# Shared expert: the last 64 gate rows and 64 up rows in one stationary operand, and TensorE's loop over tiles written out

## The chip, the core and the metric

The kernel runs on one core of one Trainium2 chip. The time is the device time of one execution in microseconds (us). Three runs of the kernel before took 1300.08, 1300.76 and 1302.69 us, median 1300.76 us. All other times below come from one profiled execution of it.

## The reference

The layer has four stages, each with a layer norm ahead of it and a residual sum behind it: a state-space mixer, a feed-forward block (FFN), a gated linear attention, and the same FFN a second time with the same weights. The FFN is where the change is:

```python
x = hidden_states.reshape(-1, H)                                        # 1024 tokens x 256
shared = _silu_and_mul(x @ shared_gate_up_w.T) @ shared_down_w.T        # 704 gate rows, 704 up rows; 704 hidden
shared = shared * jax.nn.sigmoid(x @ sgate_w.T)
routing_weights = jax.nn.softmax(x @ gate_w.T, axis=-1)                 # 16 experts
topk_w, topk_ids = jax.lax.top_k(routing_weights, TOP_K)                # 4 per token
# for each expert e: acc += silu_and_mul(x @ w13_e.T) @ w2_e.T * coef_e
out = shared + sparse_out
```

`_silu_and_mul` takes the first half of the rows as gate g, the second half as up u, and gives silu(g) * u. All of it is float32.

## The kernel before

The five instruction streams (SP for DMA issue, POOL = GpSimd, ACT = ScalarE, DVE = VectorE, PE = TensorE) are written by hand, one function for each stage and engine, and keep order among each other by counting semaphores. Float32 products with full accuracy are made of three matmuls: each operand is split into a rounded high part and a low rest, and `mm3` adds hi*hi, hi*lo and lo*hi into one PSUM bank.

**The shared expert.** The 704 hidden rows are cut into tiles of 128 (`S_TILES` = 6); 704 = 5.5 x 128, so the sixth tile (number 5) is half empty and is filled up with zero rows. The tokens are cut into two chunks of 512. For each tile and chunk PE computes the gate product into PSUM bank c and the up product into bank 2 + c, each by 2 (halves of the 256 features) x 3 matmuls of 128x512 (`f_up_pe`, L1084; `f_up_part_pe`, L1078). ACT takes silu of the gate bank into `f_s` (L1288), DVE multiplies by the up bank into `f_h` (L1545), ACT rounds it to `fh_hi`, DVE makes the rest `fh_lo` (L1549), and PE multiplies with the down weights: 4 blocks of 128 tokens x 3 matmuls of 128x256 for each tile and chunk, summed over the six tiles in banks 4 to 7 (`f_down_pe`, L1095). Up of tile i + 1 runs on PE before down of tile i. Tiles 0 and 1 are written out among the routing's matmuls; tiles 2 to 5 are two rounds of a hardware loop (`pe.Fori`, L1071).

**Routing and experts.** Beside it DVE computes which tokens go to which expert. With that POOL scatters the token rows into slots in DRAM by 32 indirect DMAs (L1335, destination `slots_d`), SP waits for their landing and loads the slots back tile by tile (`xg`, L1579), and PE works through 47 tiles of tokens (`f_experts_pe`, L1106): transpose (L1147), up (L1170), transpose of the hidden (L1183), down (L1195). SP waits for 8 scatters more ahead of each of tiles 0 to 3, so tile 3 is loaded only when all 32 have landed. PE's order puts the transpose of tile t + 1 ahead of up of tile t, so tile 3's transpose (row L1147) stands ahead of everything else of tiles 2 and later. Behind the experts come the residual sum and the next stage, or the end.

Of the kernel before, what the change touches and what calls it, by code (L numbers as in the profile page):

```python
# [23 lines left out]
ALU = mybir.AluOpType  # L24
ACT = mybir.ActivationFunctionType
AX_X = mybir.AxisListType.X

P = 128
BATCH, SEQ, DM = 4, 256, 256
# [3 lines left out]
CHUNKS = TOKENS // CHUNK  # L33
# [61 lines left out]
def build_layer(nc, xT, consts, a_vg, a_dt, a_heads, a_wo, a_par, ffn_w, router_w, route_c, moe_up, moe_down, b_qk, b_vo, b_conv,  # L95
                b_bg, b_par, out):
    ctx = ExitStack()
    with ctx:
        sems = {}

        def sem(name):
            if name not in sems:
                sems[name] = ctx.enter_context(nc.semaphore(name))
            return sems[name]
# [166 lines left out]
        def f32(ap):  # L271
            return ap.bitcast(F32)
# [14 lines left out]
        def at(t, *idx):  # L287

            return tuple(v[idx] for v in t[:2])
# [11 lines left out]
        def cols(c):  # L301
            return slice(c * CHUNK, (c + 1) * CHUNK)
# [119 lines left out]
        def split_hi(dst, src, hi_sem):  # L422
            return nc.scalar.copy(dst[0], src).then_inc(sem(hi_sem), 1)  # L423
# [632 lines left out]
        def f_pe(pe, n, f):  # L1056

            f_up_part_pe(pe, 0, 1, 1).then_inc(sem("f_up_done"), 1)
            f_up_pe(pe, f, 1, [0])

            routed(pe, "dve", f, "sofar")
            nc.tensor.matmul(ps[:, COUNT_BANK, COUNTS], ones, sofar[:, :, BLOCKS - 1], start=True, stop=True,
                             skip_group_check=True).then_inc(sem("f_route_pe"), 1)
            nc.tensor.matmul(ps[:, ROUTE_BANK, RANKS], after, mask, start=True, stop=False, skip_group_check=True)
            nc.tensor.matmul(ps[:, ROUTE_BANK, RANKS], ones, sofar[:].rearrange("p e b -> p b e"), start=False, stop=True,
                             skip_group_check=True).then_inc(sem("f_route_pe"), 1)
            f_down_pe(pe, f, 0, [0])
            f_up_pe(pe, f, 1, [1])
            routed(pe, "dve", f, "ranks_read")
            f_down_pe(pe, f, 0, [1])  # L1070
            with pe.Fori(0, S_TILES // 2 - 1) as pair:  # L1071
                for j in range(2):
                    f_up_pe(pe, f, 2 * pair + 2 + j, p=j)
                    f_down_pe(pe, f, 2 * pair + 1 + j, p=1 - j)
            f_down_pe(pe, f, S_TILES - 1)
            f_experts_pe(pe, f)

        def f_up_part_pe(pe, p, c, s):  # L1078

            for k in range(KT):  # L1080
                ins = mm3(ps[:, 2 * s + c, :], at(fgu, slice(None), p, k, s), at(xn, slice(None), k, cols(c)), k == 0, k == KT - 1)
            return ins

        def f_up_pe(pe, f, i, chunks=range(CHUNKS), p=None):  # L1084

            first = isinstance(i, int) and i == 0
            gu_split(pe, f, i)
            for c in chunks:
                if not first:
                    pe.wait_ge(sem("f_h"), HIDDENS * f + 2 * i + c - 1)  # L1090
                for s in range(2):
                    ins = f_up_part_pe(pe, i % 2 if p is None else p, c, s)
                ins.then_inc(sem("f_up_done"), 1)

        def f_down_pe(pe, f, i, chunks=range(CHUNKS), p=None):  # L1095

            p, only = (i % 2, i) if p is None else (p, None)
            d_split(pe, f, i)
            for c in chunks:
                pe.wait_ge(sem("f_h_split"), HIDDENS * f + 2 * i + c + 1)  # L1100
                for t in range(CHUNK_BLOCKS):
                    ins = mm3(ps[:, 4 + 2 * c + t // 2, t % 2 * DM:(t % 2 + 1) * DM], at(fh, slice(None), p, block_of(c, t)),
                              at(fd, slice(None), p), only == 0 and t % 2 == 0, only == S_TILES - 1)
                ins.then_inc(sem("f_down_done"), 1)

        def f_experts_pe(pe, f):  # L1106
# [178 lines left out]

        def f_silu_act(act, f, i, c):
            act.wait_ge(sem("f_up_done"), HIDDENS * f + 2 * i + c + 1)
            nc.scalar.activation(f_s[:, c], ps[:, c, :], ACT.Silu).then_inc(sem("f_silu"), 1)  # L1288

        def f_hi_act(act, f, i, c):  # L1290
            act.wait_ge(sem("f_h"), HIDDENS * f + 2 * i + c + 1)
            split_hi(at(fh, slice(None), i % 2, cols(c)), f_h[:, c], "f_h_hi")

        def f_prepare_act(act, f):
            act.wait_ge(sem("f_rw_loaded"), 16 * f + 16)
# [246 lines left out]

        def f_h_dve(dve, f, i, c):
            dve.wait_ge(sem("f_silu"), HIDDENS * f + 2 * i + c + 1)
            nc.vector.tensor_tensor(f_h[:, c], f_s[:, c], ps[:, 2 + c, :], ALU.mult).then_inc(sem("f_h"), 1)  # L1545

        def f_lo_dve(dve, f, i, c):
            dve.wait_ge(sem("f_h_hi"), HIDDENS * f + 2 * i + c + 1)
            nc.vector.tensor_tensor(fh[1][:, i % 2, cols(c)], f_h[:, c], f32(fh[0][:, i % 2, cols(c)]),  # L1549
                                    ALU.subtract).then_inc(sem("f_h_split"), 1)  # L1550

        def f_tile_sp(sp, i):
# [773 lines left out]
def _layout(i):  # L2326
    c = np.ascontiguousarray
    i = {k: np.asarray(v) for k, v in i.items()}
    w = i["L0_attn_a_W_in"]
    hn = A_HEADS * A_STATE  # L2330
    bc = w[2 * A_INNER:2 * A_INNER + 2 * hn].reshape(2, A_HEADS, A_STATE, KT, P)
    vg = w[:2 * A_INNER].reshape(2, A_TILES, P, KT, P)
    par = [i["L0_attn_a_conv_w"].reshape(A_TILES, P, A_TAPS).transpose(1, 0, 2).reshape(P, -1),
           i["L0_attn_a_conv_b"].reshape(A_TILES, P).T, i["L0_attn_a_D_param"].reshape(A_TILES, P).T,
           np.tile(i["L0_attn_a_A_log"], 4)[:, None], np.tile(i["L0_attn_a_dt_bias"], 4)[:, None]]


    gu = np.zeros((S_TILES, 2, P, DM), np.float32)
    dn = np.zeros((S_TILES, P, DM), np.float32)
    sg = i["L0_ffn_shared_gate_up_w"].reshape(2, S_HIDDEN, DM)  # L2340
    sd = i["L0_ffn_shared_down_w"].T
    for t in range(S_TILES):
        n = min(P, S_HIDDEN - t * P)
        gu[t, :, :n] = sg[:, t * P:t * P + n]
        dn[t, :n] = sd[t * P:t * P + n]
    gu = gu.reshape(S_TILES, 2, P, KT, P).transpose(0, 4, 3, 1, 2).reshape(S_TILES, P, KT * 2 * P)
    rw = np.zeros((P, DM), np.float32)
    rw[:EXPERTS] = i["L0_ffn_gate_w"]
    rw[GATE_ROW] = i["L0_ffn_sgate_w"][0]
    up = i["L0_ffn_w13"].reshape(EXPERTS, 2 * E_HIDDEN, KT, P).transpose(3, 0, 2, 1)  # L2350
    down = np.zeros((HALF_E, EXPERTS, E_STRIDE), np.float32)
    down[:, :, :2 * DM] = i["L0_ffn_w2"].reshape(EXPERTS, DM, 2, HALF_E).transpose(3, 0, 2, 1).reshape(HALF_E, EXPERTS, 2 * DM)

    qk = np.stack([i["L0_attn_b_Wq"], i["L0_attn_b_Wk"]]).reshape(2, B_HEADS, B_KD, KT, P)
    v = i["L0_attn_b_Wv"].reshape(B_HEADS, B_VT, P, DM).transpose(0, 2, 1, 3)
    cv = np.stack([i["L0_attn_b_Wq_conv"], i["L0_attn_b_Wk_conv"]]).reshape(2, B_HEADS, B_KD, P, B_TAPS)
    cb = np.stack([i["L0_attn_b_bq_conv"], i["L0_attn_b_bk_conv"]], axis=1)
    wo = i["L0_attn_b_Wo"].reshape(DM, B_HEADS, B_VT, P).transpose(1, 3, 2, 0)
    reps = P // B_HEADS
    bg = np.stack([np.tile(i["L0_attn_b_Wb"], (reps, 1)), np.tile(i["L0_attn_b_Wg"], (reps, 1))])  # L2360
    bpar = [np.tile(i["L0_attn_b_bb"], reps)[:, None], np.tile(i["L0_attn_b_bg"], reps)[:, None]]
    return dict(
        xT=c(i["L0_attn_a_x"].reshape(BLOCKS, P, DM).transpose(1, 0, 2)),
        consts=_constants(),
        a_vg=c(vg.transpose(4, 1, 3, 0, 2)),
        a_dt=c(_feature_major(np.tile(w[2 * A_INNER + 2 * hn:], (4, 1)))),
        a_heads=c(bc.transpose(1, 4, 3, 0, 2)).reshape(A_HEADS * P, KT * 2 * P),
        a_wo=c(i["L0_attn_a_W_out"].T),
        a_par=c(np.concatenate(par, axis=1)),
        ffn_w=c(np.concatenate([gu, dn], axis=2)).reshape(S_TILES * P, KT * 2 * P + DM),  # L2370
        router_w=c(rw.reshape(P, KT, P).transpose(2, 1, 0)),
        route_c=_route_constants(),
        moe_up=c(up).reshape(P, EXPERTS * E_STRIDE),
        moe_down=c(down).reshape(HALF_E, EXPERTS * E_STRIDE),
        b_qk=c(qk.transpose(1, 4, 3, 0, 2)).reshape(B_HEADS * P, QKW),
        b_vo=c(np.stack([v, wo], axis=2)).reshape(B_HEADS * P, VOW),
        b_conv=c(np.concatenate([cv.transpose(1, 3, 0, 4, 2).reshape(B_HEADS * P, CONVW), cb], axis=1)),
        b_bg=c(bg.reshape(2, P, KT, P).transpose(3, 2, 0, 1)),
        b_par=c(np.concatenate(bpar, axis=1)),
    )  # L2380
# [13 lines left out]
```

## Time and profile before

| | |
|---|---|
| device time, three runs | 1300.08, 1300.76, 1302.69 us |
| span of the profiled execution, first to last instruction | 1256.4 us |
| what lies around the span (median of the runs less that span) | 44.4 us |
| PE busy | 1205.8 us, 96% of the span |
| DVE, ACT, POOL busy | 847.7, 814.3, 773.7 us |
| first FFN: shared expert and routing, experts | 380 to 437.7 us, 437.7 to 568 us |
| second FFN: shared expert and routing, experts | 1064 to 1119.7 us, 1119.7 to 1241 us |

The profile gives the span of its execution, not that execution's device time; the rest is the difference to the median. "PEclk" in a row is the granted clock of TensorE as a share of its full 2.4 GHz, so 0.50 is 1.2 GHz. A number in square brackets behind a row is how long the engine was idle ahead of it, and on whom it waited.

### The profile page before, as it was taken

Reading aid. Unit: us, or ns where it says so; the run is one execution under the profiler, and the core shown is the slowest. Engines: PE = TensorE matmul, PEld = TensorE weight load, DVE = VectorE, ACT = ScalarE, POOL = GpSimd, SP = SyncE. Lnnn points to the kernel's source line nnn. Section 1 sums busy time; section 2 is a strip of 40 time slices with the busy share of each in tenths; the row PEclk is TensorE's granted clock in tenths of the full one; section 3 lists DMA queues with packets and bytes.
Section 4 is the critical chain, followed back from the end, with each engine's and each line's share of the span. In section 5 each row is a group of like instructions: output and inputs, shape, how many; then the busy total and the mean of one; then the engine's idle time right before and its main releaser. Section 6 shows DMA issues by size and latency. Waiting matters only on the chain. (4 is left out here: it accounts for less than half of the span.)

```text
span 1256.4 us, 23651 instructions
## 1 busy us (share of the span) xinstructions
PE 1205.8 (96%) x7571; PEld 1057.3 (84%) x7572; DVE 847.7 (67%) x2088; ACT 814.3 (65%) x1782; POOL 773.7 (62%) x648
## 2 busy tenths in 40 slices
PE   6999999999989999997999999999999998999997
PEld 5888888888877867775899999999999997877775
DVE  7777777777788533358777777777777777743335
ACT  5887777787765333343887887888888775433332
POOL 3456665667543746552677777777777764465663
PEclk9999999999999999998999999999999998999999
DMA  3355745754215957761222232222122211776666
GB/s 114 86 145 152 206 108 164 185 144 124 54 49 162 328 123 128 138 131 61 64 66 62 61 72 75 58 71 63 58 58 62 63 20 43 254 264 115 112 116 145
DMA packets 94279, 141.60 MB, mean 113 GB/s; under 512 B 8184, under 2 KB 73976, under 8 KB 93048
## 3 DMA queue, kind: packets, MB, share of 16 engines
q1 hardware_dynamic: 74400, 102.32, 29.6%
q0 software_dynamic: 15744, 20.98, 9.8%
q10 hardware_dynamic: 4056, 17.30, 4.1%
q8 instruction: 42, 0.69, 0.2%
q14 instruction: 37, 0.30, 0.1%
HBM read 99.71 MB, written 40.86 MB: 112 GB/s over the span
## 5 line engine op out<-in xcount | busy, mean ns | idle before, releaser
L1341 POOL DMA_INDIRECT sums_d<-e_y,xg x88 | 137.2, 1560 | 98.3 <-DMA sums_d<-e_y,xg 45.0
L427 POOL TENSOR_TENSOR ms_a<-m_a,ms_a 128x384 fp32r<-128x384 f32 x128 | 130.2, 1017 | 97.5 <-ACT ms_a L423 97.3
L1462 DVE COPY e_hT<-ps 88x256 f32<-88x256 f32 x94 | 39.5, 420 | 136.3 <-PE ps L1183 134.8
L1170 PE MATMUL ps<-w,e_xT 128*128 (+1 forms) x376 | 127.6, 462 | 1.5 <-ACT e_xT L1255 1.0
L894 DVE TENSOR_TENSOR m_a<-ps,e_a 128x384 f32<-128x384 f32 x128 | 71.2, 557 | 67.2 <-PE ps L278 66.2
L276 PE MATMUL ps<-xn_hi,aw_hi 128*128 128x512 f32 x256 | 107.0, 418 | 1.0 <-DVE bmat_lo L817 1.0
L278 PE MATMUL ps<-xn_hi,aw_lo 128*128 128x512 f32 x256 | 101.0, 395 | 0.0
L277 PE MATMUL ps<-xn_lo,aw_hi 128*128 128x512 f32 x256 | 100.8, 394 | 0.0
L427 POOL TENSOR_TENSOR qk_lo<-qf,qk_hi 128x512 fp32r<-128x512 f32 x64 | 84.4, 1340 | 25.2 <-ACT qk_hi L423 23.6
L427 POOL TENSOR_TENSOR ms_b_lo<-m_b,ms_b_hi 128x384 fp32r<-128x384 f32 x64 | 65.2, 1019 | 52.4 <-ACT ms_b_hi L423 52.4
L1195 PE MATMUL ps<-w,e_hT 88*128 (+1 forms) x376 | 96.7, 379 | 0.0
L1335 POOL DMA_INDIRECT slots_d<-rows,slot_i x64 | 66.0, 1031 | 42.8 <-DVE slot_i L1527 23.9
L427 POOL TENSOR_TENSOR planes_lo<-qsum,planes_hi 128x256 fp32r<-128x256 f32 x64 | 57.8, 904 | 47.6 <-ACT planes_hi L1829 47.0
L1170 PEld LDWEIGHTS ps<-w,e_xT 128*128 128x128 f32 x376 | 64.0, 190 | 23.2 <-issue 2.0
L423 ACT CAST ms_a<-m_a 128x384 fp32r<-128x384 f32 x128 | 64.9, 507 | 23.7 <-DVE m_a L894 22.6
L1262 ACT ACTIVATE e_s<-ps 128x176 f32<-128x176 f32 x94 | 29.8, 318 | 74.2 <-PE ps L1170 74.2
L827 DVE SCALAR_TENSOR_TENSOR e_a<-rows_a,ncum_a,ps 128x128 f32<-128x128 f32 x256 | 76.6, 341 | 1.9 <-DMA rows_a<-a_rows_d 1.0
L1272 ACT COPY e_y<-ps 128x256 f32<-128x256 f32 x88 | 32.8, 372 | 67.5 <-PE ps L1195 55.2
L276 PE MATMUL ps<-fold_hi,xn_hi 128*128 128x256 f32 x256 | 73.3, 286 | 1.1 <-ACT q L1820 1.1
L276 PE MATMUL ps<-planes_hi,wconv_hi 128*128 128x260 f32 (+1 forms) x256 | 73.3, 286 | 0.2 <-DVE conv_y L1988 0.2
L278 PE MATMUL ps<-planes_hi,wconv_lo 128*128 128x260 f32 (+1 forms) x256 | 73.0, 285 | 0.0
L277 PE MATMUL ps<-planes_lo,wconv_hi 128*128 128x260 f32 (+1 forms) x256 | 72.9, 285 | 0.0
(311 smaller groups left out, 4524.2 us busy)
## 6 DMA issues: line engine op xcount, KB each, us to landing
rows_a<-a_rows_d SPq DMA_DIRECT2D x64, 256.0 KB, 4.8
xg<-slots_d SPq DMA_DIRECT2D x94, 144.0 KB, 2.4
slots_d<-slot_init SPq DMA_DIRECT2D x10, 1152.0 KB, 6.6
w<-moe_up ACTq DMA_DIRECT2D x8, 1408.0 KB
wconv_raw<-b_conv SPq DMA_DIRECT2D x16, 513.0 KB, 3.6
aw_raw<-a_heads SPq DMA_DIRECT2D x32, 256.0 KB, 2.8
wvo_raw<-b_vo SPq DMA_DIRECT2D x16, 512.0 KB, 3.3
rows_b<-b_rows_d SPq DMA_DIRECT2D x32, 256.0 KB, 4.8
```

Of the source, the lines that this page charges most:

```text
L276: nc.tensor.matmul(o, w[0], v[0], start=first, stop=False, skip_group_check=True)
L277: nc.tensor.matmul(o, w[0], v[1], start=False, stop=False, skip_group_check=True)
L278: return nc.tensor.matmul(o, w[1], v[0], start=False, stop=last, skip_group_check=True)
L423: return nc.scalar.copy(dst[0], src).then_inc(sem(hi_sem), 1)
L427: return nc.gpsimd.tensor_tensor(dst[1], src, f32(dst[0]), ALU.subtract).then_inc(sem(done_sem), 1)
L827: ins = nc.vector.scalar_tensor_tensor(e[:, d * P:(d + 1) * P], row[:, d * P:(d + 1) * P], ncum[:, 2 * b + d, bass.ds(h, 1)], causal_ps, A ...
L894: nc.vector.tensor_tensor(m_a[:, b, :], ps[:, 4 + b, 0:TRI], e_a[:, b, :], ALU.mult).then_inc(sem("a_m_done"), 1)
L1170: ins = nc.tensor.matmul(ps[:, 2 + t % 2, 0:2 * E_HIDDEN], e_xT[:, t % 2, k], weights_of(w13, t, at_w, k * 2 * E_HIDDEN, 2 * E_HIDDEN), st ...
L1195: ins = nc.tensor.matmul(ps[:, 6 + t % 2, 0:DM], e_hT[0:HALF_E, t % 2, j], weights_of(w2[0:HALF_E], t, at_w, j * DM, DM), start=j == 0, st ...
L1335: nc.gpsimd.indirect_dma_start(slots_d[f], bass.IndirectOffsetOnAxis(ap=slot4_i[:, b, k:k + 1], axis=0), rows[:, b, :], None).then_inc(sem ...
L1341: nc.gpsimd.indirect_dma_start(sums_d[f][t % CHAINS], bass.IndirectOffsetOnAxis(ap=xg[:, t % XG, ROW_ID:ROW_ID + 1].bitcast(U32), axis=0), ...
L1462: nc.vector.tensor_copy(e_hT[0:HALF_E, t % 2], ps[0:HALF_E, 4 + t % 2, 0:2 * P].rearrange("p (j m) -> p j m", j=2)).then_inc(sem("e_hT"), 1)
```

## The change

Tile 5 now has no zero rows in its up weights. Its 64 gate rows and 64 up rows are put side by side in the first of the two stationary operands of that tile, so that one product gives gate in partitions 0 to 63 of bank c and up in partitions 64 to 127 of the same bank. PE issues 6 matmuls for each chunk of that tile instead of 12. ACT's silu reads partitions 0 to 63 and writes `f_s` at 64 to 127; DVE multiplies partitions 64 to 127 of `f_s` and of the bank, and the two splits work on partitions 64 to 127 too. The 64 down rows move to partitions 64 to 127, with zeros ahead; the down matmuls stay 128x256 and as many as before. Since the last tile is not like the others any more, PE's loop over tiles 2 to 5 is replaced by the same steps written out.

```diff
-            with pe.Fori(0, S_TILES // 2 - 1) as pair:
-                for j in range(2):
-                    f_up_pe(pe, f, 2 * pair + 2 + j, p=j)
-                    f_down_pe(pe, f, 2 * pair + 1 + j, p=1 - j)
+            for i in range(2, S_TILES):
+                f_up_pe(pe, f, i)
+                f_down_pe(pe, f, i - 1)
             f_down_pe(pe, f, S_TILES - 1)
...
-                for s in range(2):
-                    ins = f_up_part_pe(pe, i % 2 if p is None else p, c, s)
+                for s in range(1 if i == S_TILES - 1 else 2):
+                    ins = f_up_part_pe(pe, i % 2, c, s)
...
-            nc.scalar.activation(f_s[:, c], ps[:, c, :], ACT.Silu).then_inc(sem("f_silu"), 1)
+            nc.scalar.activation(f_s[f_rows(i), c], ps[0:HP if i == S_TILES - 1 else P, c, :], ACT.Silu).then_inc(sem("f_silu"), 1)
+
+        def f_rows(i):
+
+            return slice(HP, P) if i == S_TILES - 1 else slice(0, P)
...
-            split_hi(at(fh, slice(None), i % 2, cols(c)), f_h[:, c], "f_h_hi")
+            split_hi(at(fh, f_rows(i), i % 2, cols(c)), f_h[f_rows(i), c], "f_h_hi")
...
-            nc.vector.tensor_tensor(f_h[:, c], f_s[:, c], ps[:, 2 + c, :], ALU.mult).then_inc(sem("f_h"), 1)
+            r = f_rows(i)
+            nc.vector.tensor_tensor(f_h[r, c], f_s[r, c], ps[r, c if i == S_TILES - 1 else 2 + c, :], ALU.mult).then_inc(sem("f_h"), 1)
...
+    gu[S_TILES - 1, 0] = sg[:, S_HIDDEN - HP:].reshape(P, DM)
+    dn[S_TILES - 1, HP:] = sd[S_HIDDEN - HP:]
```

On PE, in the first FFN, the loop was entered behind the last down matmul of tile 0 like this (`fgu` are the up weights, `xn` the normed tokens; what a row waits for stands behind it):

```order
L278 MATMUL ps<-fd_hi,fh_lo 128x256
L1071 UNCONDITIONAL_BRANCH
L1071 ISA
L1090 ISA [waits f_gu_split_dve]
L276 MATMUL ps<-xn_hi,fgu_hi 128x512 [waits f_h]
L277 MATMUL ps<-xn_lo,fgu_hi 128x512
```

The branch, the loop's register and the separate waiting instruction are gone; the first up matmul now waits for both semaphores itself. Inside the loop the second chunk of an odd tile (3, then 5) had 12 matmuls:

```order
L276 MATMUL ps<-xn_hi,fgu_hi 128x512 [waits f_h]
L277 MATMUL ps<-xn_lo,fgu_hi 128x512
L278 MATMUL ps<-xn_hi,fgu_lo 128x512
L276 MATMUL ps<-xn_hi,fgu_hi 128x512
L277 MATMUL ps<-xn_lo,fgu_hi 128x512
L278 MATMUL ps<-xn_hi,fgu_lo 128x512
L276 MATMUL ps<-xn_hi,fgu_hi 128x512
L277 MATMUL ps<-xn_lo,fgu_hi 128x512
L278 MATMUL ps<-xn_hi,fgu_lo 128x512
L276 MATMUL ps<-xn_hi,fgu_hi 128x512
L277 MATMUL ps<-xn_lo,fgu_hi 128x512
L278 MATMUL ps<-xn_hi,fgu_lo 128x512
```

In the changed kernel the second chunk of tile 5 stands on PE with 6 matmuls, and down of tile 4 follows:

```order
L276 MATMUL ps<-xn_hi,fgu_hi 128x512 [waits f_h]
L277 MATMUL ps<-xn_lo,fgu_hi 128x512
L278 MATMUL ps<-xn_hi,fgu_lo 128x512
L276 MATMUL ps<-xn_hi,fgu_hi 128x512
L277 MATMUL ps<-xn_lo,fgu_hi 128x512
L278 MATMUL ps<-xn_hi,fgu_lo 128x512
L276 MATMUL ps<-fd_hi,fh_hi 128x256 [waits f_h_split,f_d_split_dve]
```

Down of tile 4, down of tile 5 and the experts' first transposes stand 12 matmuls nearer in each FFN. On ACT the order is unchanged; the last tile's rows read, in the changed kernel:

```order
L1213 DMA w_208<-moe_down 88x4x512
L1287 ACTIVATE f_s<-ps 64x512 [waits f_up_done] x2
L423 CAST fh_hi<-f_h 64x512 [waits f_h] x2
L1254 COPY e_xT<-ps 128x256 [waits e_turned,f_route_dve]
L1254 COPY e_xT<-ps 128x256 [waits e_turned]
```

Only the height of the two middle rows has changed from 128 to 64 partitions.

## Rows read from the trace of the kernel before

**Rows 1.** The page: busy time, share of the span and instructions of each engine.
```profile
PE 1205.8 (96%) x7571; PEld 1057.3 (84%) x7572; DVE 847.7 (67%) x2088; ACT 814.3 (65%) x1782; POOL 773.7 (62%) x648
```

**Rows 2.** Chain that ended last, second FFN: start, us, what.
```profile
1121.67 2.66 DMA slots_d<-rows,slot_i
...
1126.49 0.44 PE ps L1147 x2
```

**Rows 3.** Timeline of PE, first FFN: start, us, instruction, [idle before <-releaser].
```profile
426.39 0.39 PE L276 MATMUL ps<-xn_hi,fgu_hi 128*128 128x512 f32 x1
...
431.98 0.28 PE L276 MATMUL ps<-fd_hi,fh_hi 128*128 128x256 f32 x1
...
437.73 0.60 PE L1147 MATMUL ps<-const,xg 128*128 128x128 f32 x4
...
439.91 0.43 PE L1147 MATMUL ps<-const,xg 128*128 128x128 f32 x2
...
441.37 0.38 PE L1183 MATMUL ps<-const,e_h 128*88 128x128 f32 x2
444.43 0.44 PE L1147 MATMUL ps<-const,xg 128*128 128x128 f32 x2 [2.68 <-DMA xg<-slots_d]
```

**Rows 4.** Timeline of POOL and of SP's queue, first FFN.
```profile
439.66 0.96 POOL L1335 DMA_INDIRECT slots_d<-rows,slot_i  x1 [0.30 <-issue]
...
435.06 0.32 SPq L1579 DMA_DIRECT2D xg<-slots_d  x1
...
442.48 1.75 SPq L1579 DMA_DIRECT2D xg<-slots_d  x4
```

**Rows 5.** Timeline of PE, second FFN.
```profile
1122.58 0.44 PE L1147 MATMUL ps<-const,xg 128*128 128x128 f32 x2 [0.49 <-DMA xg<-slots_d]
...
1126.49 0.44 PE L1147 MATMUL ps<-const,xg 128*128 128x128 f32 x2 [2.06 <-DMA xg<-slots_d]
```

**Rows 6.** Who PE waited for, 444 to 570, then 1126 to 1252: us, times, longest.
```profile
PE ps L1147 <- DMA xg<-slots_d: 3.3, 2, 2.7
...
PE ps L1147 <- DMA xg<-slots_d: 2.1, 1, 2.1
```

**Rows 7.** Timeline of PE around the loop's way back, first FFN.
```profile
417.82 0.28 PE L278 MATMUL ps<-fd_hi,fh_lo 128*128 128x256 f32 x1
417.94 0.39 PE L276 MATMUL ps<-xn_hi,fgu_hi 128*128 128x512 f32 x1
```

**Rows 8.** Two copies at 32 partitions, two shared-expert steps at 128: ns min/median/max.
```profile
L1284 ACT COPY lgT<-ps x2: 558/566/575, 381.3 to 1063.8; 32x512 f32<-32x512 f32 x2
L1288 ACT ACTIVATE f_s<-ps x24: 589/598/601, 385.9 to 1114.2; 128x512 f32<-128x512 f32 x24
L1366 DVE COPY lgT<-ps x2: 678/678/679, 387.3 to 1069.5; 32x512 f32<-32x512 f32 x2
L1545 DVE TENSOR_TENSOR f_h<-f_s,ps x24: 679/681/690, 386.5 to 1115.9; 128x512 f32<-128x512 f32 x24
```

**Rows 9.** Timeline of PE: three waits in other stages.
```profile
573.80 1.94 PE L342 MATMUL ps<-const,rows 128*128 128x128 f32 x8 [5.47 <-DVE rows L409]
616.71 0.72 PE L276 MATMUL ps<-xn_hi,wqk_hi 128*128 128x512 f32 x1 [1.87 <-ACT q L1820]
1060.83 0.76 PE L281 MATMUL ps<-xn_hi,rw_hi 128*128 128x512 f32 x1 [0.77 <-ACT xn_hi L374]
```

**Rows 10.** Windows: length, PE busy (instructions), PEclk, DMA share, GB/s.
```profile
446.00:448.00 2.00, 2.00 (x12) 1.00 0.13 46
1126.00:1128.00 2.00, 1.51 (x7) 1.00 0.90 258
579.00:579.50 0.50, 0.50 (x3) 0.73 0.00 0
617.00:617.50 0.50, 0.50 (x2) 0.50 0.39 156
1063.50:1064.00 0.50, 0.50 (x3) 0.54 0.00 0
```

More of the change, by code:

```diff
@@ L1082, in f_up_part_pe, with f_up_pe @@
             return ins
-        def f_up_pe(pe, f, i, chunks=range(CHUNKS), p=None):
+        def f_up_pe(pe, f, i, chunks=range(CHUNKS)):
             first = isinstance(i, int) and i == 0
@@ L1090, in f_up_pe, with f_down_pe @@
                     pe.wait_ge(sem("f_h"), HIDDENS * f + 2 * i + c - 1)
-                for s in range(2):
-                    ins = f_up_part_pe(pe, i % 2 if p is None else p, c, s)
+                for s in range(1 if i == S_TILES - 1 else 2):
+                    ins = f_up_part_pe(pe, i % 2, c, s)
                 ins.then_inc(sem("f_up_done"), 1)
-        def f_down_pe(pe, f, i, chunks=range(CHUNKS), p=None):
-            p, only = (i % 2, i) if p is None else (p, None)
+        def f_down_pe(pe, f, i, chunks=range(CHUNKS)):
+            p = i % 2
             d_split(pe, f, i)
@@ L1102, in f_down_pe @@
                     ins = mm3(ps[:, 4 + 2 * c + t // 2, t % 2 * DM:(t % 2 + 1) * DM], at(fh, slice(None), p, block_of(c, t)),
-                              at(fd, slice(None), p), only == 0 and t % 2 == 0, only == S_TILES - 1)
+                              at(fd, slice(None), p), i == 0 and t % 2 == 0, i == S_TILES - 1)
                 ins.then_inc(sem("f_down_done"), 1)
@@ L1544, in f_h_dve @@
             dve.wait_ge(sem("f_silu"), HIDDENS * f + 2 * i + c + 1)
-            nc.vector.tensor_tensor(f_h[:, c], f_s[:, c], ps[:, 2 + c, :], ALU.mult).then_inc(sem("f_h"), 1)
+            r = f_rows(i)
+            nc.vector.tensor_tensor(f_h[r, c], f_s[r, c], ps[r, c if i == S_TILES - 1 else 2 + c, :], ALU.mult).then_inc(sem("f_h"), 1)
         def f_lo_dve(dve, f, i, c):
             dve.wait_ge(sem("f_h_hi"), HIDDENS * f + 2 * i + c + 1)
-            nc.vector.tensor_tensor(fh[1][:, i % 2, cols(c)], f_h[:, c], f32(fh[0][:, i % 2, cols(c)]),
+            r = f_rows(i)
+            nc.vector.tensor_tensor(fh[1][r, i % 2, cols(c)], f_h[r, c], f32(fh[0][r, i % 2, cols(c)]),
                                     ALU.subtract).then_inc(sem("f_h_split"), 1)
@@ L2341, in _layout @@
     sd = i["L0_ffn_shared_down_w"].T
[L2342 to L2345, printed above, removed]
+    for t in range(S_TILES - 1):
+        gu[t] = sg[:, t * P:(t + 1) * P]
+        dn[t] = sd[t * P:(t + 1) * P]
+    gu[S_TILES - 1, 0] = sg[:, S_HIDDEN - HP:].reshape(P, DM)
+    dn[S_TILES - 1, HP:] = sd[S_HIDDEN - HP:]
     gu = gu.reshape(S_TILES, 2, P, KT, P).transpose(0, 4, 3, 1, 2).reshape(S_TILES, P, KT * 2 * P)
```

## The prediction

> **What bounds the kernel now.** I read the busy shares first. PE is busy 96% of the span [rows 1], so 24 matmuls less look like time saved. The share is a mean over stages, though, and the question is which wait ends last behind the shared expert. So next came the chain that ended last, around the second FFN: 32 scatters of POOL, the landing of the last one, the load of a token tile, and only then PE [rows 2]. PE's shared-expert matmuls are not in it. For the first FFN the chain has no pieces, so there I read the timelines. PE ends the shared expert at 437.73, runs the first two expert tiles as far as it may, and then stands 2.68 us, until 444.43, for tile 3 [rows 3]. That tile's load is the first of the four that SP issues from 442.48, behind the last scatter (POOL 439.66 + 0.96 = 440.62) and its landing [rows 4]. In the second FFN PE waits 0.49 us for tile 2 and 2.06 us for tile 3 [rows 5]. Both FFNs are thus held by routing, POOL and DMA, and PE is early by 2.68 us in the one and 2.06 us (2.55 with both waits) in the other.
>
> Behind these waits PE does set the end: over the rest of the experts it waits for a token tile only once more, 3.3 - 2.7 = 0.6 us in the first FFN, and in the second not at all [rows 6]. So what is saved ahead of tile 3's wait is lost in it, and what is lost behind it counts in full.
>
> **Part 1: 12 matmuls less in each FFN.** Up of tile 5 runs from 426.39 to 431.98, where down of tile 4 follows without a gap [rows 3]: 5.59 us for 24 matmuls, 0.233 us each. Half of them go: 12 x 0.233 = 2.80 us for one FFN, 5.59 us for both. PE then reaches the experts at 437.73 - 2.80 = 434.93. Tile 2's transpose can move from 439.91 at most to 437.11; its load is issued at 435.06 [rows 4], so it may become a short wait of its own, which changes nothing behind it. Tile 3 is where it was, at 444.43. PE stands idle from 441.37 + 0.38 - 2.80 = 438.95 on, so 2.68 us become 5.48 us. In the second FFN 0.49 becomes 3.29 us and 2.06 stays. Nothing that the scatters wait for has moved: they depend on logits, counts and ranks, all ahead of the changed code. Gain on the path: 0 of 5.59 us.
>
> **Part 2: the loop written out.** At the loop's way back the next up matmul begins at 417.94, 0.12 us behind the last down matmul at 417.82, with no idle time beside it [rows 7]. Taking the branch away gives 0. The Trainium skill (Runtime: NRT & Kernel Launch, "Instruction fetch mechanics") says that a taken branch whose target lies outside the engine's small instruction window stalls the engine for a fetch. By that rule PE would gain a fetch in each FFN; this case's row shows no such stall here, and the measurement decides. The other way round, written-out code has more instructions to fetch while the weights of the experts load. No row prices that. It is at least nothing, and it would have to exceed 5.48 us in the first FFN or 2.06 + 3.29 = 5.35 us in the second before the end sees it. I take 0.
>
> **Part 3: half-height steps.** Silu, product and the two splits of tile 5 run on 64 partitions instead of 128. Rows of another height bound them: at 32 partitions and the same 512 columns ACT's copy takes 566 ns against 598 for its silu, and DVE's copy 678 against 681 for its product [rows 8]. So height hardly sets the time: between 0 and 0.03 us less each, and I take 0. They all start 2.80 us earlier with the matmul that releases them and stay as far ahead of down of tile 5 as now. Reading gate and up from one bank adds no wait, since silu and product of a chunk already follow each other. If a step took even 1 us longer, the wait at tile 3 would cover it.
>
> **Part 4: the longer idle time and TensorE's clock.** This is the one term that can reach the end. In this execution 2.68 us of idle time left the clock at 1.00 (446 to 448), and the pair of waits in the second FFN did too [rows 10]. Elsewhere 1.87 us of idle time ahead of 616.71 was followed by 0.50 [rows 9, 10]. A wait of 5.47 us, the twin of the new 5.48 us, ends at 573.80 with the clock at 0.50, and the row at 579.0 to 579.5, mean 0.73, puts its return at 579.27: 5.47 us of work at 1.2 GHz instead of 2.4. If PE sets the pace, half of that is lost, 2.7 us. The row of 0.54 at 1063.5 to 1064.0 puts another return at 1063.96, 3.13 us behind 1060.83: 1.6 us lost. A fall of the clock behind tile 3's wait thus costs 1.6 to 2.7 us, 2.1 in the middle.
>
> The Trainium skill (TensorE: Matmul & The Clock Gate, Part 1, "What's actually happening") adds that the monitor's clock runs freely and does not restart with a kernel, so where it switches differs from run to run. No single trace can show that; it agrees with a wait of 1.87 us that lost the clock beside one of 2.68 us that kept it, and by that rule the kernel before pays in some of its runs as well.
>
> What counts is the difference. In the first FFN the changed kernel should pay nearly always; of the kernel before I say half of the executions, since its wait is longer than one that lost the clock but kept it here. That is 2.1 x 1/2 = 1.05 us. In the second FFN both kernels have the 2.06 us wait last, and I take 0, with up to 2.7 us as its other end. As bounds: 0 if both pay alike, 2.7 + 2.7 = 5.4 us if the changed kernel pays twice and the one before never.
>
> **Sum.** Span 1256.4 + 44.4 around it = 1300.8; 0 for matmuls, loop and half-height steps; + 1.05 for the clock: 1301.8 us. The span's rest is taken from the median of the runs, so the sum stands on that median.
>
> **The rivals.**
>
> *The matmuls show at the end (faster).* If something that I take for fixed follows PE (the landing of the scatters, or SP's loads through less pressure on the DMA queues), one stage's or both stages' 2.80 us come back: 1298.0 or 1295.2 us. For it speaks that PE is the busiest engine; against it that no DMA is removed and that both tiles 3 were loaded late while PE stood. Chance 0.12.
>
> *The clock falls behind both waits, and seldom did before (slower).* The place is tile 3's transpose in each FFN, the price 1.6 to 2.7 us each, so 3.1 to 5.4 us together: 1303.9 to 1306.2 us. It decides from the point where PE's idle time in the stage is long enough to lose the clock each time; the twin of 5.47 us speaks for the first FFN, and the profiled execution kept its clock in both. Against it: the kernel before probably pays in part of its runs, and its three times differ by 2.6 us, as much as one such price. Chance 0.26.
>
> *The change does not shorten PE's work (fetch of the longer code, or half-height steps that run late).* Down of tile 5 would then end where it did and the time is 1300.8; were the stall longer than the cover of about 5.4 us, it would be slower by the rest, 1302 or more. Nothing in the profile speaks for it. Chance 0.04, counted as slower.
>
> *My forecast*, no change but for a share of the clock: 0.58.
>
> **How the numbers follow.** A difference under 0.2%, 2.6 us, is about what a measurement of this kernel cannot tell from no change. My forecast's own range is 1299.5 to 1303.5 us, all within it. Faster is the first rival, 0.12. Slower is the second, 0.26, less a little for its lower end within reach of the bound, and the third, so 0.28. Same is the rest, 0.60. For 8 times in 10 I go from 1299.0, which leaves most of the first rival out, to 1305.6, which takes in the second up to near its upper end.
>
> **What would show it.** In the changed kernel's trace: tile 5's up takes 2.80 us, the experts' first transposes begin 2.8 us earlier against the scatters, the wait ahead of tile 3 grows to 5.5 us in the first FFN, and a wait of about 3.3 us stands ahead of tile 2 in the second; the last scatter and the load of tile 3 stand where they stood. The clock is 0.50 behind tile 3's wait in the first FFN, for 3 to 6 us. I am wrong if tile 3's load comes earlier by microseconds, if PE shows gaps in tiles 2 to 5 of the shared expert, or if the clock falls twice and the runs of the kernel before never pay.

## The result and the profile after

The changed kernel is faster. Nineteen runs of it took 1286.83 to 1303.22 us, median 1294.34 us; nineteen of the kernel before took 1298.65 to 1307.22 us, median 1302.69 us. The ratio is 0.9935 (95% interval 0.9918 to 0.9953), the difference of the means 8.2 +- 2.2 us. The forecast of 1301.8 us and its range from 1299.0 us missed it, and faster had been given 0.12.

The page of the changed kernel's profile, its span and the row that answers to [rows 1]:

```profile
span 1295.7 us, 23573 instructions
PE 1207.9 (93%) x7547; PEld 1056.0 (81%) x7548; DVE 847.6 (65%) x2088; ACT 814.0 (63%) x1782; POOL 770.2 (59%) x648
```

This execution's own device time is known: 1297.55 us. So only 1.85 us lie around its span, not 44.4, and its span is 39.3 us longer than that of the kernel before although the kernel is faster. PE's busy time is the same within 0.2%. A second profile of the kernel before (experiment 1) has a span of 1295.0 us in 1296.92 us. The execution that the prediction was read from was an unusual one: with 1.85 us around it, it would have taken 1258 us, and the fastest timed run of the kernel before in this whole study took 1288.97 us.

What the ordinary executions have and the unusual one lacks is seen in PE's waits of the changed kernel from 376 to 470 us (columns: who waited, for what, us in total, times, longest):

```profile
PE ps L278 <- issue: 8.9, 7, 2.4
PE ps L276 <- issue: 6.2, 4, 1.7
PE ps L277 <- issue: 6.2, 4, 2.4
```

"issue" means that no release stands in the profile just ahead of the instruction. No wait for a token tile is in the full list: the 2.68 us of [rows 3] are gone, where the prediction had 5.48 us. The timeline of PE, which answers to [rows 3], shows where these 21.3 us lie:

```profile
415.25 0.49 PE L278 MATMUL ps<-xn_hi,fgu_lo 128*128 128x512 f32 x1
...
417.36 0.28 PE L278 MATMUL ps<-fd_hi,fh_lo 128*128 128x256 f32 x1 [1.12 <-issue]
...
437.80 0.37 PE L278 MATMUL ps<-fd_hi,fh_lo 128*128 128x256 f32 x1 [2.43 <-issue]
439.90 0.37 PE L276 MATMUL ps<-fd_hi,fh_hi 128*128 128x256 f32 x1 [1.73 <-issue]
442.70 0.37 PE L277 MATMUL ps<-fd_lo,fh_hi 128*128 128x256 f32 x1 [2.43 <-issue]
443.42 0.58 PE L278 MATMUL ps<-fd_hi,fh_lo 128*128 128x256 f32 x1 [0.34 <-issue]
...
453.66 0.39 PE L276 MATMUL ps<-xn_hi,fgu_hi 128*128 128x512 f32 x1
...
456.45 0.28 PE L276 MATMUL ps<-fd_hi,fh_hi 128*128 128x256 f32 x1
...
462.20 0.60 PE L1146 MATMUL ps<-const,xg 128*128 128x128 f32 x4
```

From about 416 to 443.4 PE executes a down matmul every 0.7 to 2.8 us, with a few closer together, instead of every 0.12 us. I call this **the stall**. Behind it PE runs the rest of the shared expert without a gap: tile 5's up now takes 456.45 - 453.66 = 2.79 us, as worked out, and the experts begin at 462.20, when the load of tile 3 has long been issued (POOL's last scatter, ACT's silus and SP's queue, which answer to [rows 4] and [rows 8]):

```profile
398.06 1.24 POOL L1338 DMA_INDIRECT slots_d<-rows,slot_i  x1 [11.99 <-DVE slot_i L1530]
...
437.97 0.96 POOL L1338 DMA_INDIRECT slots_d<-rows,slot_i  x1 [0.30 <-issue]
```
```profile
419.83 0.61 ACT L423 CAST fgu_hi<-fw_raw 128x512 fp32r<-128x512 f32 x1
441.31 0.60 ACT L1287 ACTIVATE f_s<-ps 128x512 f32<-128x512 f32 x1 [20.86 <-remote]
...
455.25 0.59 ACT L1287 ACTIVATE f_s<-ps 64x512 f32<-64x512 f32 x1 [0.88 <-PE ps L278]
```
```profile
440.42 2.49 SPq L1584 DMA_DIRECT2D xg<-slots_d  x5
```

POOL's scatters go on at their usual pace through the stall, ACT stands for 20.86 us. The stall begins some 17 us behind the first scatter's begin and ends 443.4 - (437.97 + 0.96) = 4.5 us behind the last one's issue, or 443.4 - 440.4 = 3.0 us behind the landing that lets SP load tile 3.

What ACT waits for can be read. Its silu of a chunk waits for nothing but a semaphore that PE raises with the last up matmul of that chunk. For the second chunk of tile 3 that matmul is the one at 415.25 above; here are the silu in the changed kernel, then matmul and silu of the same chunk in the first profile of the kernel before:

```profile
443.53 0.60 ACT L1287 ACTIVATE f_s<-ps 128x512 f32<-128x512 f32 x1 [1.62 <-remote]
```
```profile
414.85 0.39 PE L278 MATMUL ps<-xn_hi,fgu_lo 128*128 128x512 f32 x1
415.28 0.60 ACT L1288 ACTIVATE f_s<-ps 128x512 f32<-128x512 f32 x1 [1.99 <-PE ps L278]
```

Without the stall the silu begins 0.04 us behind the matmul's end (414.85 + 0.39). With it, 443.53 - 415.74 = 27.8 us pass, and for the first chunk 28.7 us. The trace has an update of this semaphore 0.02 us ahead of each of the two silus, and the profile calls its raiser "remote" because it finds no instruction that raises it then. So PE's signals reach ACT up to 29 us late, and DVE waits for ACT in turn (20.8 us at the longest). Why PE itself issues slowly, this does not show. The window (length, PE, PEld, DVE, ACT, POOL busy with counts, clock, DMA share, GB/s) of the changed kernel, and the same window of the first profile of the kernel before:

```profile
415.00:443.00 28.00, 6.72 (x22) 5.11 (x21) 1.80 (x3) 1.52 (x3) 18.29 (x19) 0.57 0.45 159
1115.00:1143.00 28.00, 8.07 (x20) 5.14 (x20) 0.69 (x1) 0.97 (x2) 17.69 (x19) 0.56 0.45 154
```
```profile
415.00:443.00 28.00, 26.45 (x162) 22.70 (x160) 13.24 (x27) 9.12 (x19) 19.83 (x20) 1.00 0.86 301
```

22 matmuls stand against 162, POOL's scatters are 19 against 20, and the DMA engines move half as much. The granted clock is 0.57 on the mean in place of 1.00. In the chain that ended last, from 1112 to 1165 us in the changed kernel, the shares are these; the landing of scatters and the token tile of [rows 2] have left it, and PE's matmuls behind the stall have come in:

```profile
by line: issue 37.8%; PE ps L276 18.7%; PE ps L277 18.2%; PE ps L278 17.3%; PE ps L1169 5.5%; PE ps L1146 1.3%; ACT e_xT L1254 0.7%; PE ps L1182 0.5%; ACTq L1251 0.0%
```

### The profile page after: what moved, and what is told of

Same layout as the page of the kernel before. It is cut to its first block and busy times, and to the rows that moved or that the text cites. A ratio compares the mean times of both kernels' runs of the same rounds, so it can differ in the third digit from the quotient of the medians.

```text
span 1295.7 us, 23573 instructions
## 1 busy us (share of the span) xinstructions
PE 1207.9 (93%) x7547; PEld 1056.0 (81%) x7548; DVE 847.6 (65%) x2088; ACT 814.0 (63%) x1782; POOL 770.2 (59%) x648
## 5 line engine op out<-in xcount | busy, mean ns | idle before, releaser
L1338 POOL DMA_INDIRECT slots_d<-rows,slot_i x64 | 63.2, 987 | 42.8 <-DVE slot_i L1530 23.9
L427 POOL TENSOR_TENSOR planes_lo<-qsum,planes_hi 128x256 fp32r<-128x256 f32 x64 | 57.7, 901 | 47.0 <-ACT planes_hi L1834 46.3
```

Of the source, the lines that this page charges most:

```text
L427: return nc.gpsimd.tensor_tensor(dst[1], src, f32(dst[0]), ALU.subtract).then_inc(sem(done_sem), 1)
L1338: nc.gpsimd.indirect_dma_start(slots_d[f], bass.IndirectOffsetOnAxis(ap=slot4_i[:, b, k:k + 1], axis=0), rows[:, b, :], None).then_inc(sem ...
```

## The experiments

Twelve experiments ran, in three groups (1 to 4, 5 to 8, 9 to 12), each group on one chip beside its own runs of the kernel before (medians 1296.63, 1298.93 and 1301.93 us). Differences of means are given with a 95% interval.

**1. The kernel before, profiled again** (no edit).

> The kernel before, unchanged, one more profile. The changed kernel's trace shows TensorE issuing one matmul in 1 to 3 us for some 28 us of each shared expert (415 to 443 and 1116 to 1143 us), the profile of before that the prediction was read from does not, and its span was 44 us under the times of its runs. Theory A (an ordinary execution of the kernel before has that stall too, and the profile I read was an execution without it): span 1297 to 1305 us, about 20 us longer in each FFN than in the profile I read, and a clock of 0.50 in each stall. Theory B (the stall belongs to the changed kernel alone, and the 44 us lie outside the span): span about 1256 us again, no stall.

Measured: 1296.92 us, span 1295.0 us. Its window and PE's timeline:

```profile
418.00:444.00 26.00, 12.22 (x29) 5.78 (x27) 1.98 (x3) 1.72 (x3) 17.00 (x18) 0.62 0.38 137
1118.00:1144.00 26.00, 8.80 (x22) 4.53 (x20) 2.67 (x4) 2.09 (x4) 17.03 (x18) 0.61 0.39 139
```
```profile
379.11 0.77 PE L281 MATMUL ps<-xn_hi,rw_hi 128*128 128x512 f32 x1 [0.77 <-ACT xn_hi L374]
...
443.99 0.79 PE L278 MATMUL ps<-xn_hi,fgu_lo 128*128 128x512 f32 x1 [0.81 <-issue]
...
460.33 0.60 PE L1147 MATMUL ps<-const,xg 128*128 128x128 f32 x4
...
1079.72 0.77 PE L281 MATMUL ps<-xn_hi,rw_hi 128*128 128x512 f32 x1 [0.77 <-ACT xn_hi L374]
...
1162.82 0.60 PE L1147 MATMUL ps<-const,xg 128*128 128x128 f32 x4
```

The stall belongs to the kernel before as well. From the router's first matmul (operand `rw_hi`) to the experts 81.2 and 83.1 us pass in the two FFNs; in the first profile it was 59.1 and 58.9. I call this time **the shared expert's time**. So in an ordinary run PE comes late, some 16 us behind tile 3's data, and the 12 matmuls lie behind the stall.

**2 and 7. The loop alone.** The loop is written out, tile 5 stays as before with 24 matmuls.

```diff
-            with pe.Fori(0, S_TILES // 2 - 1) as pair:
-                ...
+            for i in range(2, S_TILES):
+                f_up_pe(pe, f, i)
+                f_down_pe(pe, f, i - 1)
```

> The kernel before with TensorE's loop over tiles 2 to 5 written out, and nothing else; tile 5 keeps its 24 matmuls. Theory A1 (TensorE's work behind the stall sets the end, so the 12 matmuls less in each FFN are the whole gain, and the loop is free): 1302.7, no difference to the kernel before, ratio 0.998 to 1.002. Theory A2 (the loop's own instructions, its branch, register arithmetic and separate waits, are dear while TensorE's instructions come slowly): 2 to 4 us faster, ratio 0.997 or less. Theory C (the longer code costs fetches): slower.

> The kernel before with the loop written out, again, on the chip of this call, to set apart what the loop and what the 12 matmuls are worth. Theory A1: no difference to the kernel before, and 5.6 us slower than the changed kernel. Theory A2 (the loop's own instructions cost in the stall): 2 to 4 us faster than the kernel before.

Measured: ratio 0.9989 (0.9968 to 1.0011) on one chip, 0.9981 (0.9953 to 1.0009) on the other; differences -1.2 +- 2.4 and -3.5 +- 2.5 us (the second without one run of 3051.6 us, which the median of 1297.3 us hardly feels). Neither ratio is told from 1. Weighted together the differences make -2.3 +- 1.7 us, so a small gain is likelier than none. The expectation of no difference (A1) and that of 2 to 4 us (A2) are both still possible.

**3 and 8. The changed kernel, on the same two chips** (no edit).

> The changed kernel again, on the same chip as the others of this call. Expected from its 19 runs: ratio 0.992 to 0.995, 6 to 11 us faster than the kernel before. Theory A1: 5.6 us below loop written out alone (two times 12 matmuls of 0.233 us), more where the clock is 0.50. Theory A2: about 5.6 us below it too, but 8 us below the kernel before.

> The changed kernel on the chip of this call. Theory A1 and A2: 5 to 9 us faster than the kernel before, ratio 0.993 to 0.996.

Measured: medians 1291.79 and 1294.71 us, ratios 0.9975 (0.9950 to 0.9999) and 0.9957 (0.9929 to 0.9985), differences -4.0 +- 2.5 and -5.4 +- 2.9 us. With the first comparison's -8.2 +- 2.2 the weighted mean is -6.1 +- 1.4 us. The 24 matmuls that went make 5.59 us by the prediction's own working. Against the loop alone, though, the changed kernel is ahead by only 2.8 +- 2.8 and 1.9 +- 3.2 us, weighted 2.4 +- 2.1 us, which leaves the expected 5.6 us out. The profiles agree: the shared expert's time is 79.9 to 81.3 us with the loop alone (four FFNs) and 77.1 to 83.6 us in the changed kernel (six). So the sum fits, but that the 24 matmuls count in full is not shown, and the split between tile 5 and the loop stays open.

**4. Scatters behind the shared expert.** POOL waits for the last down product before its first scatter.

```diff
+            pool.wait_ge(sem("f_down_done"), HIDDENS * (f + 1))
             for i, k in enumerate(reversed(range(TOP_K))):
```

> The changed kernel with GpSimd's 32 scatters of an FFN held until TensorE has ended the shared expert. Theory D (the stall is tied to the scatters: it comes while they and their landings run): no stall in the shared expert, which ends some 50 us behind its start as in the profile I read (about 437 us in the first FFN), and TensorE then waits some 40 us for the scatters; span 1300 to 1345 us. Theory E (the stall comes from something else in that stretch, the weights' loads or the code): the stall stays in the shared expert, and the span grows by 35 us or more over the changed kernel's.

Measured: 1328.55 us. No stall is left in the shared expert, whose time in the first FFN is about 56.3 us, the first profile's 59.1 less the 2.8 of tile 5. What takes its place is seen in PE's waits of the first FFN:

```profile
PE ps L1146 <- DMA xg<-slots_d: 38.2, 4, 14.7
```

The stall is tied to the scatters: with none in flight, the same instructions of PE and ACT run at full pace.

**5. 24 filler matmuls** behind the shared expert of the changed kernel, in each FFN.

```diff
             f_down_pe(pe, f, S_TILES - 1)
+            keep_busy(pe, 24, 3)
```

> The changed kernel with 24 idle matmuls (zeros, 128x512, into a free bank) on TensorE behind each FFN's shared expert, ahead of the experts: 24 x 0.22 = 5.2 us of work for each FFN. Theory A1 (in an ordinary execution TensorE's work behind the stall sets when the experts begin): 10 us slower than the changed kernel of this call, ratio to it 1.008. The forecast's theory (tile 3's load comes late, some 5 us of cover in each FFN): no difference, ratio 1.000.

Measured: 1302.07 us, 8.6 +- 3.5 us above the changed kernel on the same chip by the means (ratio to the kernel before 1.0021, 0.9995 to 1.0047). In the prediction's picture 5.2 us of fillers in each FFN would have vanished in tile 3's wait. Of the 10.4 us in both, 8.6 show: PE sets the end there.

**6. A pause behind 16 scatters.** In the changed kernel, behind the second of the four groups of 8, POOL waits until both have landed.

```diff
                                                  rows[:, b, :], None).then_inc(sem(f"slots_stored{i}"), 16)
+                if i == 1:
+                    for j in range(2):
+                        pool.wait_ge(sem(f"slots_stored{j}"), 16 * BLOCKS * (f + 1))
```

> The changed kernel with one wait more on GpSimd: behind the 16th of the 32 scatters of each FFN it waits until all 16 have landed. Theory D1 (the stall comes when scatters that are under way have piled up, about 15 to 17 scatters in): no stall, or a much shorter one late in the second half; the last scatter is some 4 us later, the experts begin at 448 to 452 us instead of 459 to 462 in the first FFN; about 15 to 25 us faster than the changed kernel, 1270 to 1280 us. Theory D2 (the stall comes from a time or a place in the code, not from the number of scatters under way): the stall stays, its end moves with the last scatter, 4 us later in each FFN: about 8 us slower.

Measured: 1274.53 us, ratio to the kernel before 0.9806 (0.9767 to 0.9845). That is 19.9 +- 4.2 us ahead of the changed kernel on the same chip, as expected for D1. POOL, and PE beside it:

```profile
418.61 0.96 POOL L1338 DMA_INDIRECT slots_d<-rows,slot_i  x1 [0.30 <-issue]
421.80 0.96 POOL L1338 DMA_INDIRECT slots_d<-rows,slot_i  x1 [2.23 <-DMA slots_d<-rows,slot_i]
```
```profile
420.62 0.58 PE L277 MATMUL ps<-fd_lo,fh_hi 128*128 128x256 f32 x1 [1.14 <-issue]
...
441.00 0.55 PE L276 MATMUL ps<-fd_hi,fh_hi 128*128 128x256 f32 x1 [4.32 <-issue]
```
```profile
415.00:443.00 28.00, 21.77 (x120) 18.93 (x119) 9.34 (x15) 8.28 (x15) 19.52 (x20) 0.90 0.82 288
```

A pause of 2.23 us ended a stall that had begun. The 16 scatters behind it brought a shorter one, a gap of 4.32 us near their end (6.04 us in the second FFN), and the shared expert's time is 67.0 and 68.8 us, still 11 to 12 us above the 56.3 of experiment 4. In the stall's window PE executes 120 matmuls instead of 22 beside as many scatters, and the DMA engines move 288 GB/s instead of 159. So neither POOL's work nor the DMA engines' load alone is the cause; what differs is how many scatters follow each other without a wait.

That they pile up, as the expectation has it, the packets do not show. The DMA queue of the scatters moves 1536 packets for 32 of them, 48 each. From 395 to 424 us it moved 864 in the changed kernel, so 18 of the 20 scatters begun, and 730 in the first profile of the kernel before, so 15 of 19. With the stall fewer scatters were under way than without it.

**9 and 10. Pauses behind scatters 12 and 24**, in the changed kernel and in the kernel before.

```diff
+                    if (i, b) in ((1, 3), (2, 7)):
+                        for j in range(i):
+                            pool.wait_ge(sem(f"slots_stored{j}"), 16 * BLOCKS * (f + 1))
+                        pool.wait_ge(sem(f"slots_stored{i}"), 16 * (BLOCKS * f + b + 1))
```

> The changed kernel with two waits on GpSimd, behind the 12th and the 24th scatter of each FFN, each until all scatters so far have landed. Theory D1 (the stall comes some 16 scatters into an unbroken run of them, and a pause ends it): no stall at all; the last scatter some 4 to 5 us later than 440, the experts held by tile 3's load at about 448 us; 25 to 30 us faster than the kernel before, a few us better or worse than the single pause. Theory D2 (it depends on the time or place): the stall stays.

> The kernel before with the same two waits. With the stall gone, the prediction's own sum should hold: the loads behind the scatters end last, and the 12 matmuls less in each FFN are lost in the wait for tile 3. Then this kernel is within 0.2% of the changed one with the same waits. Theory A1 extended (TensorE sets the end even without the stall): 5.6 us, 0.4%, slower than it.

Measured: 1279.16 us with the change, 1278.0 without it; ratios to the kernel before 0.9820 (0.9796 to 0.9844) and 0.9811 (0.9784 to 0.9839). The changed kernel is 1.1 +- 2.7 us behind, so the 5.6 us of A1 are left out: with most of the stall gone the change is worth nothing that can be measured. A part of the stall is left, against the expectation: the shared expert's time is 63.0 and 64.7 us with the change, 63.0 and 62.0 without. PE's waits from 395 to 470 us, with the change and without:

```profile
PE ps L1146 <- DMA xg<-slots_d: 8.5, 1, 8.5
```
```profile
PE ps L1147 <- DMA xg<-slots_d: 7.0, 1, 7.0
```

Here tile 3's wait exists. In the second FFN it is 6.2 and 8.6 us, so in every FFN it is over twice the 2.80 us of the 12 matmuls and can swallow them, as the prediction had it. The 2.80 us themselves are not seen in the waits, since what is left of the stall differs by as much.

**11. A gap without a wait.** Twelve small memsets behind the sixteenth scatter, meant to space the scatters without waiting for their landing.

```diff
+                if i == 1:
+                    for j in range(12):
+                        nc.gpsimd.memset(gap[:, 16 * j:16 * (j + 1)], 0.0)
```

> The changed kernel with 12 small memsets on GpSimd behind the 16th scatter of each FFN, so a gap in the scatters without any wait for their landing. Theory D3 (the gap itself lets the other engines on): a shorter stall that begins again later, and a gain of 5 to 20 us over the changed kernel. Theory D1 (what matters is that the scatters under way have landed): the stall stays as it is, no gain, or 2 us lost.

Measured: 1295.56 us, ratio 0.9951 (0.9931 to 0.9971), within the range of the changed kernel's 0.9935 to 0.9975; the stall is there. The memsets made a much shorter gap than the pause of experiment 6:

```profile
418.56 0.96 POOL L1339 DMA_INDIRECT slots_d<-rows,slot_i  x1 [0.31 <-issue]
419.52 0.63 POOL L1343 MEMSET gap<- 128x16 f32 x12
420.32 0.97 POOL L1339 DMA_INDIRECT slots_d<-rows,slot_i  x1 [0.16 <-issue]
```

So 0.8 us without a landing don't help. Whether 2.2 us without one would is open, and the experiment decides less than it was to.

**12. A pause behind each group of 8**, in the changed kernel.

```diff
+                if i < TOP_K - 1:
+                    pool.wait_ge(sem(f"slots_stored{i}"), 16 * BLOCKS * (f + 1))
```

> The changed kernel with a wait on GpSimd behind the 8th, 16th and 24th scatter of each FFN. Theory D1: no stall; three waits of 2 to 3 us put the last scatter at 446 to 449 us, so this is 3 to 6 us slower than the two waits of the other kernel of this call, and about 20 to 25 us faster than the kernel before.

Measured: 1280.0 us, ratio 0.9839 (0.9804 to 0.9874). PE's shared expert runs at full pace here:

```profile
409.00:435.00 26.00, 25.49 (x156) 22.89 (x157) 13.71 (x25) 10.16 (x19) 11.45 (x12) 1.00 0.89 290
```

Its time is 56.5 and 56.4 us, as in experiment 4, and the silus of the last three tiles begin within 0.2 us of PE's signal. So the stall goes by the length of the run: 77 to 84 us of shared expert with 32 scatters unbroken (eight profiles; the first one, with 59, is the exception), 67 to 69 with 16, 62 to 65 with 12, 56 with 8. The price is that the three pauses put the last scatter's end at 452.2 us instead of 442.2 with one pause, and PE waits 12.1 us for tiles in the first FFN. With 12 scatters in the window where the first profile has 20, the lower rate may have a part in the full pace. By their ratios one pause, two and three are not told apart (0.9806, 0.9811 to 0.9820, 0.9839).

## Why the prediction was wrong

**The failed step is the first: what bounds the kernel now.** The sum took "span 1256.4 + 44.4 around it". The 44.4 us do not lie around a span; in every run here whose span is known the device time exceeds it by 1.75 to 3.5 us. They lie inside an ordinary execution, in the two shared experts: these take (81.2 - 59.1) + (83.1 - 58.9) = 46.3 us longer in experiment 1, of which 7.7 us come back elsewhere, since the spans differ by 38.6 us. The profile that was read had no stall, so PE came early there and, without pauses or late scatters, late everywhere else. The prediction named this sign itself: it is wrong "if PE shows gaps in tiles 2 to 5 of the shared expert".

**Part 1, the matmuls.** The size was right: 2.80 us worked out, 2.79 read. "Gain on the path: 0 of 5.59 us" was wrong, since the cover, tile 3's wait, doesn't exist in an ordinary run. In all eight profiles that have the stall in full it ends 1.8 to 3.0 us behind the landing of the last scatter (by SP's load of tile 3), whatever PE has done by then, and all that is left of the shared expert runs behind it. Experiment 5 shows that work there counts; experiments 9 and 10 show that the prediction's cover is there as soon as most of the stall is taken away. How much of the gain is the matmuls' own is not settled (experiments 3 and 8). The first rival, "the matmuls show at the end", came out near the measured time, 1295.2 us for both stages, but by luck: nothing came to follow PE through less pressure on queues. In ordinary runs PE had been the bound all along.

**Part 2, the loop.** Forecast 0, measured -2.3 +- 1.7 us over two chips, not told from 0 on either alone. Where no stall covers the loop's way back (the first profile and experiment 10) PE goes over it at its usual 0.12 us; in experiment 1 it lies in the stall, and what the loop costs there no row shows. The Trainium skill's rule (Runtime: NRT & Kernel Launch, "Instruction fetch mechanics"), by which a taken branch to a place outside the engine's instruction window costs a fetch, would give a gain this sign; no run here shows such a fetch, nor that the loop's start lies outside.

**Part 3, the half-height steps.** Right: the silu on 64 partitions took 0.59 us beside 0.60 on 128.

**Part 4, the clock.** The second rival asked for a fall of the clock behind tile 3's wait. That wait is gone, and the granted clock falls in the stall of both kernels, where PE executes one matmul in a microsecond or more (means 0.62 and 0.61 before, 0.57 and 0.56 after; 0.50 in the changed kernel from 430 to 443), and is back at 1.00 before the experts begin. It doesn't separate the kernels, and the term of 1.05 us has no place. Where the wait does exist the price was right: in experiments 9 and 10 PE stands 6.2 to 8.6 us for tile 3, and the clock is 0.50 for 3.2 to 5.0 us behind each of the four waits, which by the prediction's reckoning costs half of that, 1.6 to 2.5 us, in both kernels alike.

**The spread.** Runs of one kernel differ by up to 16 us here. Where the stall catches PE differs from one profile to the next: 76 to 112 of the shared expert's matmuls were left behind it, in the profiles of both kernels and of the loop alone. At 0.12 to 0.23 us each that makes a spread of this kind: the changed kernel's profile with 217 left in both FFNs took 1297.55 us, that with 168 left 1291.85 us. It is argued from eight profiles, not shown for each run.

## What to carry to other kernels

Before a wait in a profile is used as cover, compare the profiled span with the run times: here a remainder of 44 us where others have 2 was time that an ordinary execution spends inside its span, and the wait read as cover did not exist there. When an engine starts late, look up the instruction that raises its semaphore, too: here it had ended up to 29 us before. Experiments that add work (fillers) or take a suspect away (late scatters) tell who sets the end. One wait for the landing half-way through a long run of indirect scatters was worth 20 us here, over three times the change under study (6.1 us).

## What the runs showed of the hardware

PE and ACT nearly cease to execute (22 matmuls in 28 us instead of 162) while GpSimd issues its 32 indirect scatters without a wait, from about the fifteenth to seventeenth on until 3.3 to 4.5 us behind the last one's issue, 25 to 28 us in each FFN. ACT then waits for semaphores that PE should have raised up to 29 us before; PE's own gaps have no releaser in the profile. The signal that comes 28.7 us late belongs to a matmul that ends at 412.57, ahead of PE's first gap at 416.3.

The stall shrinks with the number of scatters between two waits for their landing: the shared expert loses 21 to 27 us to it with 32, 11 to 12 us with 16, 3 to 8 us with 12, and nothing with 8. A gap of 0.8 us without a wait does nothing. The DMA engines are less busy in the stall (share 0.38 to 0.45) than in the same window without it (0.86 in the first profile), and in the changed kernel's first FFN no instruction packet is in flight in it (the nearest of their queue begin at 399.9 and 450.8 us), so both DMA bandwidth and the loading of instructions are unlikely causes.

Which resource holds PE and its signals up stays open, as does why one execution of the kernel before was free of it. One rival is untested: the recording itself may take part. The first profile gives a landing time for the scatters (5.1 us in the median), while every other profile lacks too many of these landings to give one, so it differs from the others in what was recorded; and no run with a known span is without a recording.
